# Three-stage attention, scan and expert kernel on one core: another order of VectorE's, ScalarE's and TensorE's work inside the scans

## The reference, cut to what matters

```
x = x + conv_attention(group_norm(x))          # softmax attention over 1024 pixels
t = tokens of x                                # 8 batches x 1024 tokens x 128
t = t + mamba(layer_norm(t))                   # the scans, below
t = t + experts(layer_norm(t))                 # 8 experts, top 2
```

```
z, xBC, dt = split(rmsnorm(x) @ W_in)
xBC = silu(causal convolution of xBC over 4 tokens + conv_b)
xs, Bm, Cm = split(xBC)
dt  = softplus(dt + dt_bias);  dA = exp(dt * -exp(A_log))
state = state * dA_t + (dt_t * x_t) outer B_t          # along the 1024 tokens
y_t   = state @ C_t + D * x_t
out = x + rmsnorm(y * silu(z)) @ W_out
```

## Time and profile before

| | us |
|---|---|
| median of 3 runs | 996.23 (991.87 to 997.99) |
| the profiled execution's own time | 989.1 |
| its span, first to last instruction | 987.3 |
| TensorE busy (products) | 873.4, 88% |
| VectorE busy | 727.9, 74% |
| ScalarE busy | 502.2, 51% |
| GpSimd busy | 273.0, 28% |
| mean granted clock of TensorE | 0.950 |

### The profile page before, as it was taken

The page is one execution under the profiler, slowest core; times in us unless marked ns, Lnnn a source line. Parts: engine busy times, 40 slices in busy tenths (PEclk is TensorE's granted clock), DMA queues, the critical chain, the costliest instruction groups (busy, mean ns, idle before and its releaser), DMA issues.

```text
span 987.3 us, 18734 instructions
## 1 busy us (share of the span) xinstructions
PE 873.4 (88%) x7086; PEld 679.8 (69%) x7086; DVE 727.9 (74%) x1959; ACT 502.2 (51%) x740; POOL 273.0 (28%) x264
## 2 busy tenths in 40 slices
PE   3788999999989788898989797979789999999997
PEld 2556656655666666676767675757668888888887
DVE  2867678667867668576767777686868889888985
ACT  1525455545567564656565646464315544554453
POOL 0025111011000525242525252428513331233200
PEclk9979999999999789899979999989989999999999
DMA  5631011101101230303030303032000000000001
GB/s 146 187 136 22 1 22 22 22 1 22 23 1 30 45 75 1 74 2 74 2 74 2 74 1 75 2 74 66 2 1 1 22 23 22 2 22 22 23 1 43
DMA packets 30888, 36.07 MB, mean 37 GB/s; under 512 B 4560, under 2 KB 24912, under 8 KB 30800
## 3 DMA queue, kind: packets, MB, share of 16 engines
q1 hardware_dynamic: 29648, 30.68, 12.9%
q10 hardware_dynamic: 1152, 4.19, 1.2%
HBM read 21.50 MB, written 4.98 MB: 27 GB/s over the span
## 4 chain that ended last, share of the span: by engine, by line
PE 34%; DVE 18%; issue 4%; ACT 2%; POOL 2%; DVEq 0%; ACTq 0%; POOLq 0%
PE ps L1047 7%; DVE acc L1996 4%; PE ps L969 4%; PE ps L794 3%; PE ps L796 3%; PE ps L795 3%; DVE cacc L1712 2%; PE ps L960 2%; PE ps L948 2%; PE ps L953 1%; DVE dcy L1804 1%; PE ps L905 1%; PE ps L919 1%; PE ps L872 1%; PE ps L1088 1%
## 5 line engine op out<-in xcount | busy, mean ns | idle before, releaser
L1996 DVE SCALAR_TENSOR_TENSOR acc<-ps,comb,acc 128x128 f32<-128x128 f32 x512 | 139.8, 343 | 16.3 <-PE ps L1047 15.7
L1399 ACT ACTIVATE hid<-ps,b_f 128x512 f32<-128x512 f32 x128 | 87.2, 687 | 112.1 <-PE ps L796 112.0
L1047 PEld LDWEIGHTS ps<-w_f,hid 128*128 128x128 f32 x1024 | 130.6, 191 | 19.6 <-ACT hid L1399 8.1
L1047 PE MATMUL ps<-w_f,hid 128*128 128x128 f32 x1024 | 136.8, 277 | 5.2 <-ACT hid L1399 4.6
L1569 DVE TENSOR_REDUCE nmax<-ps 128x1 f32<-128x1024 f32 x64 | 78.1, 1220 | 29.8 <-PE ps L674 29.4
L1712 DVE SCALAR_TENSOR_TENSOR cacc<-ps,cw,cacc 128x1023 f32<-128x1023 f32 (+5 forms) x72 | 91.7, 1275 | 10.3 <-ACT cacc L1271 9.2
L570 POOL TENSOR_TENSOR srs<-sve,neg_half 128x1 f32<-128x1 f32 x64 | 53.8, 841 | 147.9 <-DVE gram L1821 147.8
L1187 ACT ACTIVATE probs<-ps,nmax 128x1024 f32<-128x1024 f32 x64 | 71.3, 1114 | 39.3 <-DVE nmax L1569 36.5
L969 PE MATMUL ps<-y_w 128*128 128x256 f32 x256 | 75.1, 420 | 12.8 <-DVE X L1831 12.2
L1340 ACT ACTIVATE dcy<-ps 128x1024 f32<-128x1024 f32 x64 | 65.1, 1017 | 40.8 <-PE ps L919 40.7
L1864 DVE TENSOR_TENSOR y_w<-ps,zs 128x256 f32<-128x256 f32 x64 | 27.0, 422 | 78.5 <-PE ps L960 76.0
(11 more groups left out here) (214 smaller groups left out, 1881.9 us busy)
## 6 DMA issues: line engine op xcount, KB each, us to landing
c_dec<-exp_dram SPq DMA_DIRECT2D x32, 256.0 KB, 5.1
xc<-in_x SPq DMA_DIRECT2D x8, 512.0 KB, 3.6
q_b<-q_a SPq DMA_DIRECT2D x16, 256.0 KB, 2.8
X<-in_x_tok ACTq DMA_DIRECT2D x8, 512.0 KB, 5.2
c_rep<-cacc SPq DMA_DIRECT2D x32, 128.0 KB, 5.9
out<-o_ch SPq DMA_DIRECT2D x8, 512.0 KB, 2.6
w_f<-in_w SPq DMA_DIRECT2D x2, 512.0 KB, 3.7
cst_f<-in_sel_rows SPq DMA_DIRECT2D x1, 512.0 KB, 4.3
```

What stands on the lines that cost most here:

```text
L1047: last = nc.tensor.matmul(ps[:, Y_BANKS[n], t * P:(t + 1) * P], hid[n % 2][:, t * P:(t + 1) * P], w2_f[:, e, :], start=True, stop=True)
L1399: nc.scalar.activation(hid[n % 2][:], ps[:, 4 + n % 2, :], ACT.Gelu, bias=b1_f[:, n // 2:n // 2 + 1]).then_inc(e_hidden_ready, 1)
L1996: done = nc.vector.scalar_tensor_tensor(acc[u][:, tt, :], ps[:, bank, t * P:(t + 1) * P], comb[u][:, tt, e:e + 1], acc[u][:, tt, :], ALU.m ...
```

## The change

Only tables of parts are changed, and `shortcut` can run in two parts.

- TensorE: the sums (`cumulate`) run at slot 6.5 and no longer at 7.5.
- ScalarE: the residual's scaling runs as chunks 0 to 3 at slot 4 and chunks 4 to 7 at slot 5.5, no longer whole at 6.5; softplus's Exp and Ln at 4.5 (behind the tap of group 1) and no longer at 5; `factors` at 7 and no longer at 7.5.
- VectorE: all three convolutions of group 0 in step 4, in front of `y_w`; the first two of group 1 in step 5, in front of `y_w`; both parts of softplus together behind step 5; the third convolution of group 1 in step 6; the exponents in front of `y_w` in step 7, with the first convolution of group 2 behind them; the second and third of group 2 in step 0 of the next scan, the third between the residual's sum and `y_w`.

```diff
-                        (group, (1, 1), 2, 4.5), (group, (2, 0), 2, 5.5), (group, (2, 1), 2, 5.5), (cumulate, (), 2, 7.5)]
+                        (group, (1, 1), 2, 4.5), (group, (2, 0), 2, 5.5), (group, (2, 1), 2, 5.5), (cumulate, (), 2, 6.5)]
...
-            def shortcut(b, u):
+            def shortcut(b, u, t0=0, t1=NT):
 
                 act.wait_ge(m_normed, b + 1)
-                for t in range(NT):
+                for t in range(t0, t1):
                     xb = X[:, b, t * P:(t + 1) * P]
                     last = nc.scalar.activation(xb, xb, ACT.Identity, bias=rnb[:, b, 0, t:t + 1],
                                                 scale=rp1[:, b, t:t + 1])
-                last.then_inc(m_residual_ready, 1)
+                if t1 == NT:
+                    last.then_inc(m_residual_ready, 1)
...
-            dve_parts = [("conv", (2, 3), 1, -0.25), ("ends", (), 1, 1), ("low", (), 2, 2.75), ("inner", (), 1, 3),
+            dve_parts = [("conv", (2, 2), 1, -0.25), ("conv", (2, 3), 1, 0), ("ends", (), 1, 1), ("low", (), 2, 2.75),
...
```

More of the change, by code:

```diff
@@ L1363, in _ @@
                          (high, (), 2, 2.5), (tap, (0,), 2, 3.5), (gather_b, (), 1, 3.5), (steps, (), 2, 4),
-                         (tap, (1,), 2, 4.5), (softplus, (), 2, 5), (tap, (2,), 2, 5.5), (shortcut, (), 1, 6.5),
-                         (factors, (), 2, 7.5)]
+                         (shortcut, (0, 4), 1, 4), (tap, (1,), 2, 4.5), (softplus, (), 2, 4.5), (tap, (2,), 2, 5.5),
+                         (shortcut, (4, NT), 1, 5.5), (factors, (), 2, 7)]
             def pieces(b, slot):
@@ L1778, in _ @@
             fronts = [front(b, b % 2) for b in range(B)]
-            dve_parts = [("conv", (2, 3), 1, -0.25), ("ends", (), 1, 1), ("low", (), 2, 2.75), ("inner", (), 1, 3),
[L1781 to L1784, removed]
+            dve_parts = [("conv", (2, 2), 1, -0.25), ("conv", (2, 3), 1, 0), ("ends", (), 1, 1), ("low", (), 2, 2.75),
+                         ("inner", (), 1, 3), ("conv", (0, 1), 2, 4), ("conv", (0, 2), 2, 4), ("conv", (0, 3), 2, 4),
+                         ("steps", (), 2, 4.5), ("conv", (1, 1), 2, 5), ("conv", (1, 2), 2, 5),
+                         ("softplus", (0,), 2, 5.5), ("softplus", (1,), 2, 5.5), ("conv", (1, 3), 2, 6),
+                         ("exponents", (), 2, 7), ("conv", (2, 1), 2, 7)]
             def second_front(slot):
```

## The result

The changed kernel takes 954.98 us (median of 4 runs, 954.08 to 955.94), the kernel before 994.41 beside it (median of 4, 991.87 to 997.99). The ratio is 0.961, 95% interval 0.958 to 0.964. The gain is 39.4 us, forecast 30.

The account below looks back on a forecast made before the run. Bound: engine queues meeting badly, VectorE setting the second half (y_w of step 4 to y_w of step 0'). 5.5 - 0.8 + 0.3 = 5.0 us a scan, six scans 30 us: forecast 966 us, range 954 to 984.

Parts of the forecast that it names:

- The sum of VectorE's work: Second half, y_w of step 4 to y_w of step 0': 19.8 us against 25.3, so 5.5 us less a scan.
- Softplus: Behind step 5: its first instruction no longer held by GpSimd's product on c_dec, about 1.5 us off a scan.
- The two that leave are free: Step 4: two group-0 convolutions, 2.54 us, fit into VectorE's 3.00 us idle before y_w, with 0.46 left.
- The 2.62 us and VectorE's 2.88 at the turn vanish: End of the scan: TensorE's 2.62 us idle before the gates and VectorE's 2.88 before y_w of step 0' go away.
- The clock's 0.8 a scan: Steps 7 and 0': half a step's fall of TensorE's clock charged, 0.8 us a scan, bounds 0 and 3.3.
- The residual in two parts costs nothing: ScalarE, step 4 and behind the last tap: the split scaling is hidden by idle time, costing nothing.
- group 2's silu costs 0 to 1 us: ScalarE, step 0' of the next scan: silu waits for the later convolution, costed at 0 to 1 us a scan.
- the slower case: Rival: ScalarE's late silu holds TensorE's step 2 and nothing is gained; 2.5 us a scan lost, 1011 us; chance 0.05.
- The base: Whole kernel: profiled 989.1 us less 30 gives 959; 7 below the median 996.23 taken as base, so 966.
- GpSimd no longer meets softplus: Answers the rival that GpSimd's c_dec product still holds softplus: 1.5 us a scan come back, 975 us; chance 0.10.
- It changes little: Rival: TensorE's 44.2 us busy time holds, the scan stays near 49.5 us, 1 us a scan, 990; chance 0.08.
- The clock takes it: Rival: TensorE idles 2 us, then runs two steps at lower clock every scan, 3.3 instead of 0.8; 981 us; chance 0.17.

Follow-up runs that it names:

- experiment 1: The kernel before with GpSimd's second product on c_dec at slot 4.5 instead of 5.5, so that it is over before softplus starts: 983.24 us, ratio 0.989.
- experiment 4: The changed kernel with the second and third convolutions of group 0 put back behind y_w of step 4: 991.58 us, ratio 0.998.
- 11: The kernel of experiment 4 with the decay's product of step 0' issued eight times as extra TensorE work: 974.68 us, ratio 0.981.
- Experiment 12: The changed kernel with sums, exponents and factors at their old places, plus the decay's products of steps 0' and 0' + 2 issued four times each: 956.46 us, ratio 0.964.
- experiment 2: The kernel before with the early turn alone: sums at 6.5, exponents and factors at 7, convolutions left where they were: 995.70 us, ratio 1.001.
- Kernel 6: The changed kernel with the residual's scaling whole at slot 6.5 again: 956.80 us, ratio 0.964.
- kernels 3: The changed kernel with the late turn: sums, exponents and factors put back at their old places: 968.68 us, ratio 0.975.
- kernel 5: The changed kernel with group 2's last two convolutions put back: second behind step 7, third ahead of step 0's masked decay: 972.00 us, ratio 0.981.
- 7: The changed kernel with group 2's first convolution forward at slot 6.5 and its two others ahead of step 0's masked decay: 972.65 us, ratio 0.981.

## Why the prediction was right, and where it was off

*The sum of VectorE's work: right.* The forecast added up 23.15 us before, without the wait at the turn, and 19.8 after: 3.35 less. With the clock held up, the second half went from 5.10 + 7.48 + 5.34 + 5.59 = 23.51 to 20.32: 3.2 less. Softplus gave 1.47 of it (experiment 1, forecast 1.5), the two group-0 convolutions 2.3 (experiment 4 with 11, forecast 2.54); taken one by one the parts need not add up. After came out 0.5 over 19.8, and the largest piece of it is the masked decay of step 0', 1.65 instead of 1.22 us, which starts beside GpSimd's product on `xdt`. The wait for GpSimd's root in step 7 was put at 0.5 and is 0.44.

*The two that leave are free: right.* Step 4 stayed at 7.25, and its `y_w` still waits 0.32 us for TensorE (0.46 forecast).

*"The 2.62 us and VectorE's 2.88 at the turn vanish": came true, the second for another reason.* I set 25.3 against 19.8, so these waits were booked as gain of the order. Filled with extra products, before's step 0' takes 5.59 us instead of 6.9 to 8.2, with its order untouched: the gates still wait 1.44 us for `expc` there (second scan), but `y_w` waits only 0.29. So 25.3 - 23.5 = 1.8 us of the half was TensorE at the lower clock. Experiment 12 says the same from the other side: with the clock held up, the early turn is worth 0.3 us a scan in after. (In experiment 2 it gains nothing alone, but that kernel has falls of its own.)

*The clock's 0.8 a scan: the size was right, the other end of it was left out.* This is the step that failed. I charged after with 0.8 for a fall; it pays 0.66, most of it in two falls in five scans (6.02 instead of 4.54 and 8.52 instead of 7.25). But under the clock I credited nothing for the falls that before already pays; part of them sat unseen in the 25.3. They are 2.6 us a scan, at the turn in each of these scans and on the way to step 4 in three of the five. The fall that I did read, at 494, made no step longer: step 7 of that scan took 5.35 us, as in the scans without it. The right sum is 3.61 for the order and 2.61 - 0.66 = 1.95 for the clock, together the 5.56 measured, not 5.5 - 0.8 + 0.3 = 5.0. So the order was forecast 2.2 us too high (5.5 + 0.3) and the clock had the wrong sign (-0.8 for +1.95); that the two errors nearly cancel is luck. Part of this lay in the first half, which I left almost as it was: it gained 25.34 - 24.38 = 0.96 a scan, of which the order gave 24.43 - 24.01 = 0.42 (0.3 forecast). Over scans 1 to 5 the order gave 3.6 of 5.56, about two thirds.

*The residual in two parts costs nothing, group 2's silu costs 0 to 1 us: right.* Kernel 6 and after have the same scans from the fourth on (44.3). TensorE waits for `dcy` in step 2 for 0.64 us at most in scans 1 to 5, far under the 2 us that would have shown the slower case.

*The base.* I took 989.1 - 30 and added 7 to come to the median. Of the 11.2 us between 966.2 and 954.98, 1.8 are the median of before, which with a fourth run is 994.41; 4.4 are that before's profiled execution ran 5.3 us below that median and after's only 0.9 below its own; and 5.0 are scans that gained more than I forecast (2.8 in scans 1 to 5) and one fall fewer in scan 7 (1.8).

*The rivals.* GpSimd no longer meets softplus: its first instruction takes 0.19 us all eight times. "It changes little" took TensorE's 44.2 us of busy time as a floor; at the higher clock they became 208.35 / 5 = 41.7, in a scan of 44.99. "Slower" needed sums and gates that come no earlier; they came earlier. "The clock takes it" fell for after but is what happens to its neighbours: kernels 3, 4 and 5 lose 2.6 to 4.6 us a scan to it, at 969 to 992 us. The argument against it, that only one idle stays, doesn't hold: kernel 5 has that same idle of 2.13 us and falls. That after came out nearly free of falls was not something that I could have read from the order; it was luck as well.

## What to carry to other kernels

Before pricing a change of order, split the loop's time into what the queues take and what the lower clock takes: a step that takes 7.29 us in one pass and 8.83 in the next, at a granted clock of 0.50, is the second kind, and an edit that is worth tenths on paper can give that time back or bring it on. An edit that does nothing alone may still cost much when it is taken out of the whole (the early turn: 0 alone, 14 us out of after), so each part is tried both on the kernel before and out of the kernel after. Where TensorE waits at the same place of every pass, extra products in that place are a cheap probe of whether the clock is what is lost.

## What was not expected of the hardware

- More work made the kernel faster: about 1.4 us of extra products a scan (six of 0.23 us, start to start) took kernel 5 from 972.00 to 957.21 us, and twice as many took before from 995.04 to 985.09.
- The falls repeat: in kernels 5 and 7 they come at the same two steps of every scan from the third on, while the scan's period stays within 47.76 to 47.79 us.
- The same idle of 2.13 us before the same products was followed by clock 1.00 in after's fourth scan and by 0.50 in kernel 5's; in after's own second scan an idle of 2.15 us was followed by 0.50. What decides a fall stays open; the experiments show what it costs and that work added elsewhere in the scan removes it or takes it up.
- Filling helped before only in part: its fourth scan still took 51.68 us, with a fall (0.50 from 521 to 527) in step 3, which took 10.03 us instead of 6.36.
- A fall can come with hardly any idle time close ahead of it. In kernel 5 TensorE is busy 14.65 of the 15 us up to the one on the way to step 4 (fourth scan):

```profile
505.00:520.00 15.00, 14.65 (x149) 12.51 (x148) 9.39 (x15) 9.16 (x14) 8.90 (x10) 0.98 0.01 2
```

- GpSimd's short root took 1.47 us instead of 0.55 when it ran beside the masked decay of 528.62 (after), and the decay 1.65 instead of 1.22 beside GpSimd's `xdt`: either engine can be the one that is slowed.
